# Graph attention on one core: the key sum of a pair's first group split one tile and three, and the first gathers of a pair wait for the pieces

## The reference, cut to what matters

```python
q = (x @ Wq + bq).reshape(N, 8, 16)
k = (x @ Wk + bk).reshape(N, 8, 16)
v = (x @ Wv + bv).reshape(N, 8, 16)
e = (ea @ We).reshape(-1, 8, 16)
k_e = k[src] + e
v_e = v[src] + e
alpha = einsum('ehd,ehd->eh', q[dst], k_e) / sqrt(16)
# softmax over the edges of one destination node, then
out = segment_sum(attn[:, :, None] * v_e, dst)
# then a gate between out and x @ Wskip + bskip, two layer norms, a relu and the residual
```

## Time and profile before

| | us |
|---|---|
| median of 3 runs | 2765.66 |
| lowest, highest | 2759.3, 2787.53 |
| span of the profiled execution | 2774.7 |
| busy: TensorE, VectorE, GpSimd, ScalarE | 2009.6, 1801.8, 1497.6, 1140.6 |
| GpSimd's gathers, busy and idle in front of them | 1483.1 and 1144.6 |
| VectorE idle in front of the key sums | 756.0 |

### The profile page before, as it was taken

How to read it: one execution, slowest core, us unless ns; L and a number is a source line. 1 busy time by engine, 2 the same in 40 slices (tenths; PEclk the granted TensorE clock), 3 DMA queues, 4 the chain that set the end, 5 groups by cost and what they waited for, 6 DMA issues and landing times.

```text
span 2774.7 us, 45026 instructions
## 1 busy us (share of the span) xinstructions
PE 2009.6 (72%) x11492; PEld 1805.8 (65%) x11492; DVE 1801.8 (65%) x4040; ACT 1140.6 (41%) x3750; POOL 1497.6 (54%) x1591
## 2 busy tenths in 40 slices
PE   7478888888776577667766767757687777778775
PEld 5467777777666566566665767656576667667664
DVE  7465565566666566566665667657676676777764
ACT  0133333344343344344443444434454454454455
POOL 0555555555556555565555555555555555555531
PEclk9677777777777777777777777778788777777786
DMA  8556666666655555555554655555565555555541
GB/s 308 185 165 184 176 184 183 178 180 180 172 167 167 158 159 167 154 174 165 167 167 143 176 163 167 175 149 165 164 176 167 170 176 168 169 172 180 169 123 39
DMA packets 298585, 468.47 MB, mean 169 GB/s; under 512 B 49862, under 2 KB 193034, under 8 KB 298230
## 3 DMA queue, kind: packets, MB, share of 16 engines
q1 hardware_dynamic: 222680, 259.30, 31.3%
q0 software_dynamic: 75648, 206.24, 26.2%
HBM read 414.62 MB, written 50.73 MB: 168 GB/s over the span
## 4 chain that ended last, share of the span: by engine, by line
PE 54%; issue 17%; another core or an unknown queue 13%; ACT 8%; DVE 3%; DMA 2%; ACTq 1%; POOL 0%; SPq 0%; POOLq 0%; DVEq 0%
PE sum_ps L928 18%; PE q_ps L825 12%; PE e_ps L812 10%; ACT dist_en L1046 3%; PE max_ps L841 2%; PE sum_ps L866 2%; PE sum_ps L865 2%; PE sum_ps L851 2%; PE max_ps L834 2%; PE sum_ps L850 2%; ACT hot_en L1055 1%; PE sum_ps L894 1%; PE sum_ps L895 1%; DMA xt_buf<-xT 1%
## 5 line engine op out<-in xcount | busy, mean ns | idle before, releaser
L706 POOL DMA_INDIRECT kv<-kv_tab,src_all x1568 | 1483.1, 946 | 1144.6 <-DVE kve L1373 683.8
L1373 DVE TENSOR_TENSOR kve<-kv,e_ps 128x1024 f32<-128x1024 f32 x392 | 462.2, 1218 | 756.0 <-issue 626.2
L928 PE MATMUL sum_ps<-wv,hot_en 128*128 128x136 f32 x3136 | 683.7, 394 | 15.0 <-issue 11.4
L928 PEld LDWEIGHTS sum_ps<-wv,hot_en 128*128 128x128 f32 x3136 | 626.1, 291 | 60.4 <-issue 58.5
L825 PE MATMUL q_ps<-q_win,hot_ne 128*128 128x128 f32 x3136 | 458.8, 284 | 265.2 <-issue 262.8
L825 PEld LDWEIGHTS q_ps<-q_win,hot_ne 128*128 128x128 f32 x3136 | 401.5, 197 | 281.0 <-issue 278.1
L1046 ACT ACTIVATE dist_en<-iota_n,neg_rel 128x128 bf16<-128x128 f32 x1568 | 497.7, 389 | 75.9 <-issue 75.9
L812 PE MATMUL e_ps<-we,ea 128*128 128x128 f32 x3136 | 422.6, 292 | 13.1 <-issue 7.2
L1083 ACT COPY sums<-sum_ps 128x136 f32<-128x136 f32 x392 | 98.3, 263 | 798.5 <-remote 730.6
L812 PEld LDWEIGHTS e_ps<-we,ea 128*128 128x128 f32 x3136 | 415.3, 212 | 12.7 <-issue 6.4
L834 PE MATMUL max_ps<-ident,top 128*1 128x128 f32 x196 | 65.0, 332 | 332.8 <-ACT used_b L1060 296.5
(11 more groups left out here) (136 smaller groups left out, 1573.7 us busy)
## 6 DMA issues: line engine op xcount, KB each, us to landing
ea<-eaT SPq DMA_DIRECT2D x196, 512.0 KB
row_b<-rel_row SPq DMA_DIRECT2D x196, 256.0 KB
kv<-kv_tab,src_all POOLq DMA_INDIRECT x1568
q_win<-q_tab SPq DMA_DIRECT2D x392, 64.0 KB
sum_tab<-sums SPq DMA_DIRECT2D x392, 59.5 KB
kv_tab<-tab_buf SPq DMA_DIRECT2D x33, 384.0 KB, 3.7
logit<-sum_tab SPq DMA_DIRECT2D x49, 136.0 KB
xt_buf<-xT SPq DMA_DIRECT2D x33, 192.0 KB, 4.0
```

The lines of the kernel that those rows point to most:

```text
L706: pool.indirect_dma_start(out=kv[:, s, t, :], out_offset=None, in_=kv_tab[:, :], in_offset=bass.IndirectOffsetOnAxis(ap=src_all[:, tile:ti ...
L928: mm = pe.matmul(sum_ps[u][:, 0:AC], hot_en[:, s, t, :], wv[:, s, t, :], start=(t == 0), stop=(t == TILES_G - 1))
L1373: dve.tensor_tensor(kve[:, s, :, :, :], kv[:, s, :, :].rearrange("p t (a c) -> p t a c", a=2), e4.to_broadcast([P, TILES_G, 2, C]), ALU.ad ...
```

## The change

It does two things. The key sum of a pair's first group is two operations, the first tile (128x256) and then the other three (128x768), each counted by `kve_ok`; the sum of the second group stays one operation. GpSimd's first gather of a pair waits for the first tile's sum alone, the second for the rest of that group's sum, and the first gather of the second group for the second group's sum as before. All other waits on `kve_ok` are rewritten to the new count of three per pair and mean the same as before.

```diff
+        def kve_head(q):
+            return 3 * q + 1
+
+        def kve_count(g):
+            return 3 * (g // 2) + 2 + g % 2
...
                     s = 2 * par + u
-                    if q >= 2:
-                        pool.wait_ge(kve_ok, 2 * q + u - 3)
                     for t in range(TILES_G):
+                        if q >= 2 and u == 0 and t == 0:
+                            pool.wait_ge(kve_ok, kve_head(q - 2))
+                        elif q >= 2 and t == 1 - u:
+                            pool.wait_ge(kve_ok, kve_count(2 * q + u - 4))
                         tile = (2 * q + u) * TILES_G + t
                         pool.indirect_dma_start(
...
                 if not first_use:
-                    pe.wait_ge(kve_ok, g - 1)
+                    pe.wait_ge(kve_ok, kve_count(g - 2))
...
-                dve.tensor_tensor(kve[:, s, :, :, :], kv[:, s, :, :].rearrange("p t (a c) -> p t a c", a=2),
-                                  e4.to_broadcast([P, TILES_G, 2, C]), ALU.add).then_inc(kve_ok, 1)
+                for a, b in ((0, 1), (1, TILES_G)) if u == 0 else ((0, TILES_G),):
+                    dve.tensor_tensor(kve[:, s, a:b, :, :], kv[:, s, a:b, :].rearrange("p t (a c) -> p t a c", a=2),
+                                      e4[:, a:b, :, :].to_broadcast([P, b - a, 2, C]), ALU.add).then_inc(kve_ok, 1)
...
-                dve.wait_ge(kve_ok, g + 1)
+                dve.wait_ge(kve_ok, kve_count(g))
```

More of the change, by code:

```diff
@@ L714, in _ @@
                     gather(q)
-                pool.wait_ge(kve_ok, GROUPS - 2)
+                pool.wait_ge(kve_ok, kve_count(GROUPS - 3))
                 for k in range(FK):
@@ L890, in turn_back @@
                 if back_step[u] >= PAIRS + 2:
-                    pe.wait_ge(kve_ok, GROUPS)
+                    pe.wait_ge(kve_ok, kve_count(GROUPS - 1))
                 to = back_to(u)
```

## The result

The changed kernel takes 2689.87 us (median of 4 runs, 2680.22 to 2704.62); the kernel before took 2765.15 us beside it (4 runs). The ratio on record is 0.970, with a 95% interval from 0.967 to 0.974; by the medians the kernel is 75 us (2.7%) faster where 115 were forecast. Some executions fall into a slower state, and the ratios here are the record's own estimates from the others alone, so they can differ from the quotient of two medians by up to 0.003. The profiled execution went from a span of 2774.7 to 2678.4 us, 96 us less. It was the fastest of the four runs after, while the profiled execution before lay above its median; so steps are compared span with span, and the forecast for that comparison was 122 us (2774.7 to 2653).

The account below looks back on a forecast made before the run. GpSimd's gathers and VectorE's key sums, waiting for each other in turn, were taken as the bound. 2774.7 - 150 (188 x 0.80 gained) + 28 (caught signals) = 2653 us, taken as 2650 for a median, range 2605 to 2725.

Parts of the forecast that it names:

- The loop: GpSimd and VectorE wait in turn: first group's key sum, eight gathers, about 1.9 us, key sum; steady period 13.1 us.
- Rival A: GpSimd's gathers: their end releases nothing, GpSimd only idles longer, period stays 13.1 us, about 2785 us; chance 0.09.
- The first gather's start: GpSimd's first gather starts 0.69 us after the key sum's start instead of 1.49, 0.80 us gained a pair.
- The second gather's wait: GpSimd's wait for the rest of the first group's sum is hidden, with 0.30 us to spare.
- The release: From the end of GpSimd's last gather to VectorE's next key sums, kept at 1.90 us.
- The price of caught signals: ScalarE's copy of the maximum held until the gathers end: 4.6 us lost in six pairs, 28 us allowed.
- rival B: Shorter pause not always enough; ScalarE's copy of the maximum caught in half the unit-work pairs, 2850 us; chance 0.10.
- VectorE's extra operation: One more key-sum operation a pair: 0.08 us taken, bounds 0.06 and 0.15, hidden by VectorE's idle time, nothing charged.
- Rival C: TensorE becomes the bound in pairs with unit work, which gain only 0.3 us: 2702 us; chance 0.13.

Follow-up runs that it names:

- the split alone: Changed kernel with the key sum still split, but a pair's first gather waiting for the whole first group again; ratio 1.002 to the kernel before.
- six gathers: Changed kernel fetching three of each group's four tiles from the third pair on, a quarter of the fetched rows left out; 2283.89 us, ratio 0.823 to the kernel before.
- the heads in own buffers: Changed kernel with the first two tiles of a pair's first group in a third buffer, first gather not waiting for that key sum; 2633.24 us, ratio 0.953.
- The third chip: Chip on which the table's last five kernels ran; the kernel before took 2770.91 and 2767.36 us beside them.
- rows three to six: Table rows of one chip: split without earlier gather 1.002, kernel before with later first gather 1.028, first group split in halves 0.964, changed kernel with row load earlier 0.946.
- the gather later: Kernel before, unsplit, with the gathers of both groups waiting for both key sums of two pairs ago; 2879.28 us, ratio 1.028.
- the row first: Kernel before with SyncE's load of the next destination row put right behind its load of the edge rows; 2767.97 us, ratio 0.999.
- two tiles and two: Changed kernel with the first group's key sum split into two equal halves instead of one tile and three; 2695.9 us, ratio 0.964 to the kernel before.
- pause: Changed kernel with a 128x1 memset by GpSimd behind the first four gathers of each pair; 2691.34 us, ratio 0.972 to the kernel before.
- the change again: Changed kernel, unaltered, timed a second time on the chip of the last five kernels; 2672.37 us, ratio 0.967 to the kernel before.

## Why the prediction came out as it did

**The loop: right.** Key sum of the first group, eight gathers, release, key sum. Rival A, by which the gathers' end releases nothing, is refuted from three sides: the split alone gives 1.002, six gathers shorten the period by as much as the gathers, and on one chip a first gather at 0.96 instead of 0.69 us makes the period 0.22 us longer.

**The first gather's start: right.** 0.69 us was forecast and is measured in the median. The second gather's wait stays hidden in ordinary pairs, as the sum had it, but not in every pair. Every 104th gather (it falls behind the key sums of pairs 12, 25, 38 and so on) is preceded by a longer gap, 0.54 instead of 0.30 us in the kernel before. It falls on the second gather of a pair, the one that now waits for the rest of the group's sum, and it has become 1.38 us:

```profile
1400.34 2.42 DVE L1382 TENSOR_TENSOR kve<-kv,e_ps 128x256 f32<-128x256 f32 x3 [2.98 <-issue]
...
1401.03 0.94 POOL L714 DMA_INDIRECT kv<-kv_tab,src_all  x1 [2.67 <-DVE kve L1382]
1403.35 0.94 POOL L714 DMA_INDIRECT kv<-kv_tab,src_all  x1 [1.38 <-DVE kve L1382]
...
1408.34 0.94 POOL L714 DMA_INDIRECT kv<-kv_tab,src_all  x1 [0.30 <-issue]
1409.13 1.28 DVE L1382 TENSOR_TENSOR kve<-kv,e_ps 128x256 f32<-128x256 f32 x2 [0.77 <-issue]
...
1409.84 0.24 PE L849 MATMUL max_ps<-neg_max,ones_f 1*128 1x1 f32 x1
...
1415.82 0.95 POOL L714 DMA_INDIRECT kv<-kv_tab,src_all  x1 [0.30 <-issue]
1419.06 1.22 DVE L1382 TENSOR_TENSOR kve<-kv,e_ps 128x1024 f32<-128x1024 f32 x1 [8.64 <-issue]
1419.25 0.16 ACT L1068 COPY used_b<-max_ps 128x1 f32<-128x1 f32 x1 [12.60 <-remote]
...
1420.55 0.94 POOL L714 DMA_INDIRECT kv<-kv_tab,src_all  x1 [3.79 <-DVE kve L1382]
```

At 0.84 us more in each of 13 such pairs (in the fourteenth the gap was 0.47 us) this is at most 11 us. The rows also show what a disturbed pair is. The key sum at 1409.13 started early, while gathers ran; so the next pair's gathers followed with no pause but the usual 0.30 us (why it starts early was not settled, but it does so most often in these very pairs: of the 12 pairs that are over a microsecond shorter than the median in the kernel before 7 are such 13th pairs, of the 7 in the changed one 4, and of the 16 with the heads in own buffers, where the second gather has its usual gap of 0.30 us in 13 of these 14 pairs, 2). Its second key sum stood idle for 8.64 us, and the copy of the maximum came 9.17 us after its matmul's end (1410.08). Only when the fifth gather stopped, waiting for that very key sum, did both come out, 2.3 us after the last gather's end (1416.77). A gap of 1.7 to 3.9 us in front of the fifth gather stands five times in the kernel before and six times in the changed one, all but one in each in the pair directly behind such a 13th pair.

**The release: mis-sized, and this is the term of the sum that failed.** The sum kept it at 1.90 us after the gathers. It is 2.04 us in the changed kernel and 1.92 before, 0.12 us a pair, 23 us over 188 pairs. The third chip has 1.92 us before and 1.99 and 2.04 us in the two kernels with the change, 0.07 to 0.12 us more or 13 to 23 us. On the whole it grows as the pause in front of the first gather shrinks: 1.92, 1.99 and 2.23 us for pauses of 3.41, 2.68 and 2.38 us there, and 1.71, 1.79 and 1.86 us for 4.32, 3.35 and 2.82 us on the chip of rows three to six. Why it grows was not tested. So a gain of 0.80 at the start left 0.67 us in the median period: 192 x 0.67 = 129 us instead of 150.

**The price of caught signals: the size came out by luck, the kind was wrong.** 28 us had been set aside, and the excess over the steady period rose from 33 to 61 us, by just 28. But the second profile of the changed kernel has 44, so one execution scatters by as much as the whole term. ScalarE's copy of the maximum, for which the 28 us were set aside, is late more rarely than before: by over 1.5 us after its matmul 20 times instead of 42. A copy as late as that of the earlier trace rows also costs nothing, where 4.6 us had been charged: behind the 31 copies that were 1.5 to 8 us late in the kernel before the next pair took 13.07 us in the median, behind the 11 such in the changed one 12.34. Only copies over 8 us late stand beside long pairs (11 before, 9 after), and all of them lie in pairs whose next key sum had come early, not in those of the steady form. This speaks against rival B in its place and its mechanism; its sign, pairs of 15 us and more, is there 10 times against 12 before.

What took the place of this term is the wait for destination rows, 61.0 us in 21 waits and 30.4 us in the second profile. The prediction put SyncE at nothing: it counted only what TensorE and ScalarE do in GpSimd's pause. SyncE's turn begins with the edge rows, for which it waits for the edge projection. In the kernel before it waited there for 226.9 us in 104 pairs, so it had time to spare; in the changed one it waits there for 31.4 us in 9 and in nearly every other pair comes after the projection is done:

```profile
SPq L536 <- remote: 226.9, 104, 14.8
```

```profile
SPq L542 <- remote: 31.4, 9, 15.5
```

The other kernels fit. Where this wait still comes in 45 pairs or more (the kernel before, also with the gather later or the row first, the split alone, two tiles and two) the row is hardly late, 0.3 to 2.5 us in all; where it comes in 14 or fewer and the row stands last (pause, six gathers, heads, the change again) the row is late by 30 to 205 us. The kernel before with the row moved (0.999) and the changed one with it moved (0.953 against 0.967) show that the late row belongs to the change and is worth 33 to 38 us.

Together: 129 - 28 = 101 us by the periods, 96 us by the spans, where 122 had been forecast; the release's 23 us are most of the difference. The excess in this sum is that of two single executions. From the 96 us to the 75 between the medians it is scatter of single executions: the profiled run after lies 10 us under its median, the one before above it.

**VectorE's extra operation: right.** Net 0.061 us a pair by the busy time, the lower bound of the prediction, and hidden: the split alone is within 0.5% of before. By the fixed latency of an operation in the Trainium skill ("VectorE: DVE Perf Modes", section on the TRN2 errata) the estimate was 0.16 us; the 0.061 us of this trace say that most of it did not show between operations back to back.

**Rival C: not seen.** Late pairs, with unit work, hold the period of the early ones: its median is 12.43 us in pairs 2 to 59, 12.40 in pairs 60 to 129 and 12.51 from there on.

## What to carry to other kernels

When two engines wait for each other in turn, the time from the one's start to the other's start can be shortened without less work, and splitting the producer's first operation did that here at no visible cost, where the producer has idle time; run the split without the earlier wait once, and the two are told apart. When a loop gets shorter, look at what else was done in its pause, the DMA issues of a third engine above all: their order had cost nothing before and was worth 1.4% after. A third buffer that takes the wait away entirely gained half as much again as the split.

## What had not been expected of the hardware

- Signals of TensorE are late while GpSimd's indirect DMAs follow each other at 0.30 us, even signals that nothing connects with them: the next key sum came 1.7 to 2.3 us after the last gather's end in the median of every kernel of the table. SyncE is not held but slowed. From the start of one of its register instructions to the next it takes 0.21 us in the median during the first 4 us of a run of gathers, and 0.72 us from 5 us after the run's start until 1.5 us after its end, in the kernel before as in the changed one. The last matmuls of a group come in steps of the same kind. In the kernel before, where the gathers run from 1437.93 to 1447.63:

```profile
1444.42 0.27 PE L825 MATMUL q_ps<-q_win,hot_ne 128*128 128x128 f32 x1 [0.36 <-issue]
1445.86 0.27 PE L825 MATMUL q_ps<-q_win,hot_ne 128*128 128x128 f32 x1 [1.17 <-issue]
1447.30 0.27 PE L825 MATMUL q_ps<-q_win,hot_ne 128*128 128x128 f32 x1 [1.17 <-issue]
1447.97 0.71 SPq L561 DMA_DIRECT2D sum_tab<-sums  x1
1448.68 0.71 SPq L565 DMA_DIRECT2D first_tab<-sums  x1
```

  What slows them, and whether the late signals have the same cause, was not settled. "SBUF — State Buffer" of the Trainium skill, section "Who interferes with whom", says that DMA never contends with a compute engine and that TensorE and ScalarE wait on no one. It says so of SBUF ports, so the late signals neither bear it out nor refute it, and rival A could not be derived from it.
- A pause of 4.4 us lets some key sums start before the gathers' end (periods mostly between 7.6 and 19 us in turn), so later gathers cost less than the loop says: 2879 us where the loop alone gave 2980.
- Every 104th gather, which here is the second of every 13th pair, comes 0.24 us late in the kernel before. The split alone has the same 0.24 us, though its second gather has a wait as well, one that the first gather has already met. Where the second gather waits for a later sum it is 1.08 us late with one tile and three and 0.81 us with two and two; in both it starts 3.0 us after the key sum, where it starts at 1.9 and 2.2 us in ordinary pairs. With the heads in own buffers the delay is seen in 1 of 14 places. Its cause is open.
- A 128x1 memset of GpSimd between two gathers is free: 0.11 us inside a gap of 0.30 us.
